# Softmax attentions of a decoder kernel: the last head group's scores go to three pairs of PSUM banks in turn

## The reference, cut to what matters

```python
# L0 xattn: causal self attention (512 keys) + cross attention (1024 keys), heads of 16
y = softmax(mask(q @ k.T) / sqrt(16)) @ v   +   softmax(cq @ ck.T / sqrt(16)) @ cv
x = x + y @ Wp + bp
# L1 xattn: a1 (512 keys, the mask is applied after the softmax), a2 (1024 keys), heads of 32
a = softmax(q @ k.T * 32 ** -0.5);  if causal: a = a * (key > query)
o = a @ v
```

## Time and profile before

| | us |
|---|---|
| median of 3 runs | 3880.21 |
| the runs | 3872.55, 3880.21, 3882.26 |
| the profiled execution: its time | 3883.62 |
| the profiled execution: its span in the trace | 3881.9 |
| mean granted TensorE clock | 0.933 of full speed |
| TensorE / VectorE / ScalarE / GpSimd busy | 3298.2 / 2075.1 / 1646.2 / 918.5 |

### The profile page before, as it was taken

How to read it: one execution, slowest core, us unless ns; L and a number is a source line. 1 busy time by engine, 2 the same in 40 slices (tenths; PEclk the granted TensorE clock), 3 DMA queues, 4 the chain that set the end, 5 groups by cost and what they waited for, 6 DMA issues and landing times. The chain is left out here.

```text
span 3881.9 us, 57542 instructions
## 1 busy us (share of the span) xinstructions
PE 3298.2 (85%) x22048; PEld 1811.7 (47%) x22048; DVE 2075.1 (53%) x4294; ACT 1646.2 (42%) x2481; POOL 918.5 (24%) x966
## 2 busy tenths in 40 slices
PE   6898788898897788898897788999897888985997
PEld 4325445245335545244335535254335635254997
DVE  5665754644656665635656664635656664732111
ACT  3353933343354833333344742433455642431332
POOL 1202912011203712011204622011105622023111
PEclk9999799899998899899998899999998898996999
DMA  4103012111203012011202022011212022025997
GB/s 122 56 15 82 1 47 77 37 33 45 57 13 82 1 47 93 21 38 48 62 18 65 1 47 93 21 39 47 62 44 39 1 47 92 21 88 190 327 329 243
DMA packets 250149, 270.70 MB, mean 70 GB/s; under 512 B 96198, under 2 KB 215988, under 8 KB 247572
## 3 DMA queue, kind: packets, MB, share of 16 engines
q1 hardware_dynamic: 202288, 207.46, 18.2%
q10 hardware_dynamic: 44180, 50.17, 4.1%
q0 software_dynamic: 3408, 9.34, 0.6%
HBM read 199.87 MB, written 67.05 MB: 69 GB/s over the span
## 5 line engine op out<-in xcount | busy, mean ns | idle before, releaser
L881 ACT ACTIVATE prob<-psum 128x1024 f32<-128x1024 f32 x384 | 372.3, 1021 | 514.2 <-PE psum L799 514.2
L1262 ACT ACTIVATE prob<-psum 128x1024 f32<-128x1024 f32 (+3 forms) x384 | 331.2, 914 | 363.4 <-PE psum L1151 363.4
L927 DVE TENSOR_REDUCE scr<-psum 128x1 f32<-128x512 f32 x576 | 369.5, 686 | 201.4 <-PE psum L786 197.4
L1304 DVE TENSOR_REDUCE stats<-psum 128x1 f32<-128x512 f32 (+3 forms) x576 | 332.1, 619 | 139.3 <-PE psum L1139 136.2
L796 PE MATMUL psum<-stack 32*128 32x512 f32 x1536 | 226.6, 660 | 15.2 <-ACT prob L881 10.4
L412 PE MATMUL psum<-ident 128*128 128x128 f32 x1792 | 217.9, 277 | 2.7 <-ACT stack L2229 2.7
L412 PEld LDWEIGHTS psum<-ident 128*128 128x128 f32 x1792 | 210.0, 192 | 15.0 <-issue 7.5
L1139 PE MATMUL psum<-stack 96*128 96x512 bf16 (+3 forms) x576 | 181.3, 363 | 31.5 <-DVE stats L1304 31.2
L829 PE MATMUL psum<-prob,ones_f 128*32 128x512 f32 x1536 | 204.9, 601 | 0.0
L1166 PE MATMUL psum<-prob,vbig 128*32 128x512 f32 (+3 forms) x1536 | 189.4, 566 | 0.0
L1699 POOL TENSOR_TENSOR xo<-xa,rows 128x256 f32<-128x256 f32 x32 | 22.3, 728 | 664.3 <-POOLq L1452 664.3
(11 more groups left out here) (488 smaller groups left out, 6401.5 us busy)
## 6 DMA issues: line engine op xcount, KB each, us to landing
ew<-in_L_ffn_W SPq DMA_DIRECT2D x39, 1024.0 KB
ew<-in_L_ffn_W ACTq DMA_DIRECT2D x39, 1024.0 KB
stack<-q_terms SPq DMA_DIRECT2D x144, 128.0 KB, 2.6
w_mlp<-in_L_xattn_a_li_w SPq DMA_DIRECT2D x16, 1024.0 KB, 6.5
q_terms<-parts SPq DMA_DIRECT2D x96, 128.0 KB, 2.2
stack<-k_terms SPq DMA_DIRECT2D x72, 128.0 KB, 3.0
stack<-k_terms SPq DMA_DIRECT2D x36, 256.0 KB
w_mlp<-a_terms SPq DMA_DIRECT2D x36, 256.0 KB, 4.6
```

The source lines that it names most:

```text
L881: act.activation(prob[:, i % 4, :, :], psum[:, 2 * p:2 * p + 2, :], ACT.Exp, scale=scale).then_inc(exped, 1)
L927: dve.tensor_reduce(found[:, c:c + 1], ring(i), AX.X, ALU.max).then_inc(freed, 1)
L1262: act.activation(prob[:, i % 4, :, q0:T], psum[:, 2 * p:2 * p + 2, q0:T], ACT.Exp, scale=scale).then_inc(exped, 1)
L1304: dve.tensor_reduce(found[:, c:c + 1], ring(i)[:, 0:keys_of(t)], AX.X, ALU.max).then_inc(freed, 1)
```

## The change

In the last head group of all four attentions the scores of step m (counted from the group's first) go by pairs of banks: pair (2m + p) mod 3 for the pair of heads p = 0, 1, where the pairs are banks 0-1, 2-3 and 4-5. A score of this group after its first waits for one exponential of the step before in place of two. Since banks 4 and 5 are taken by that, the products in Bca go to banks 6 and 4 in place of 4 and 5, are ordered by row tile, and are issued at other places: two each at kt = 4, 5 and 6, two before the last gather, two before the last spread, two after it, with two `keep_running` matmuls behind in place of six. They wait for the division of group 2 in place of that of group 1. Cq reads banks 6 and 4, and its transposes use banks 5 and 7.

```diff
+    def score_bank(n, j, kts):
+        m = n - (HG - 1) * kts
+        return j if m < 0 else 2 * ((2 * m + j // 2) % 3) + j % 2
+
+    def exps_before_score(n, kts):
+        return 2 * n if n <= (HG - 1) * kts else 2 * n - 1
...
                     if n:
-                        pe.wait_ge(exped, 2 * n)
+                        pe.wait_ge(exped, exps_before_score(n, kts))
...
-                        last = pe.matmul(psum[:, j, q0:T], KTg[W * j:W * j + W, g, kt * P:(kt + 1) * P],
+                        last = pe.matmul(psum[:, score_bank(n, j, kts), q0:T], KTg[W * j:W * j + W, g, kt * P:(kt + 1) * P],
...
-                    if next_products and g == HG - 1 and 3 <= kt < 7:
-                        pe.wait_ge(divided, HG - 2)
-                        for t, k in next_products[2 * kt - 6:2 * kt - 4]:
+                    if next_products and g == HG - 1 and 4 <= kt < 7:
+                        pe.wait_ge(divided, HG - 1)
+                        for t, k in next_products[2 * kt - 8:2 * kt - 6]:
                             join_attention(pe, t, k)
...
-                if next_products:
-                    pe.wait_ge(divided, HG - 1)
-                for t, k in next_products[8:10]:
+                for t, k in next_products[6:8]:
                     join_attention(pe, t, k)
                 if not next_products:
                     keep_running(pe, 3, 3)
                 gather(HG - 1)
-                for t, k in next_products[10:]:
+                for t, k in next_products[8:10]:
                     join_attention(pe, t, k)
                 if not next_products:
                     keep_running(pe, 2, 3)
                 spread_inverses(pe, HG - 1, inverted, spread_in)
-                keep_running(pe, 6, 3)
+                for t, k in next_products[10:]:
+                    join_attention(pe, t, k)
+                keep_running(pe, 2 if next_products else 6, 3)
...
-                        act.activation(prob[:, i % 4, :, q0:T], psum[:, 2 * p:2 * p + 2, q0:T], ACT.Exp,
+                        b0 = score_bank(n, 2 * p, kts)
+                        act.activation(prob[:, i % 4, :, q0:T], psum[:, b0:b0 + 2, q0:T], ACT.Exp,
...
-        return pe.matmul(psum[:, 4 + t // 2, t % 2 * C:(t % 2 + 1) * C], yT[:, k, t * P:(t + 1) * P], wBp[:, k, :],
+        return pe.matmul(psum[:, (6, 4)[t // 2], t % 2 * C:(t % 2 + 1) * C], yT[:, k, t * P:(t + 1) * P], wBp[:, k, :],
...
-                   next_products=[(t, k) for k in range(HG - 1) for t in range(QT)], beside=add_bias)
+                   next_products=[(t, k) for t in range(QT) for k in range(HG - 1)], beside=add_bias)
...
-        return psum[:, 4 + h, :].rearrange("p (t n) -> p t n", t=2)
+        return psum[:, (6, 4)[h], :].rearrange("p (t n) -> p t n", t=2)
...
-                turn(h, 6 + h).then_inc(turned, 1)
+                turn(h, 5 + 2 * h).then_inc(turned, 1)
```

More of the change, by code:

```diff
@@ L795, in score @@
                     for j in range(J):
-                        pe.matmul(psum[:, j, :], KTg[W * j:W * j + W, g, kt * P:(kt + 1) * P], QTg[W * j:W * j + W, g, :],
+                        pe.matmul(psum[:, score_bank(n, j, kts), :], KTg[W * j:W * j + W, g, kt * P:(kt + 1) * P], QTg[W * j:W * j + W, g, :],
                                   start=True, stop=False)
                     for j in range(J):
-                        last = pe.matmul(psum[:, j, :], ones_b[W * j:W * j + W, :], low[W * j:W * j + W, g % 2, :],
+                        last = pe.matmul(psum[:, score_bank(n, j, kts), :], ones_b[W * j:W * j + W, :], low[W * j:W * j + W, g % 2, :],
                                          start=False, stop=True)
@@ L880, in _ @@
                             act.wait_ge(weighed, n - 1)
-                        act.activation(prob[:, i % 4, :, :], psum[:, 2 * p:2 * p + 2, :], ACT.Exp, scale=scale).then_inc(exped, 1)
+                        b0 = score_bank(n, 2 * p, kts)
+                        act.activation(prob[:, i % 4, :, :], psum[:, b0:b0 + 2, :], ACT.Exp, scale=scale).then_inc(exped, 1)
                     if kt == order[0] and g:
@@ L2219, in _ @@
                 pe.wait_ge(normed, 2 * QT - 2 + 2 * h)
-                turn(h, 6 + h).then_inc(x_turned, 1)
+                turn(h, 5 + 2 * h).then_inc(x_turned, 1)
             e.keep_running(pe, 6, 0)
@@ L2233, in _ @@
                 act.wait_ge(turned, h + 1)
-                act.copy(xT[:, :, h * N:(h + 1) * N], psum[:, 6 + h, :].rearrange("p (k n) -> p k n", k=KT)).then_inc(xT_in, 1)
+                act.copy(xT[:, :, h * N:(h + 1) * N], psum[:, 5 + 2 * h, :].rearrange("p (k n) -> p k n", k=KT)).then_inc(xT_in, 1)
             for h in range(2):
                 act.wait_ge(x_turned, h + 1)
-                act.copy(xT[:, :, h * N:(h + 1) * N], psum[:, 6 + h, :].rearrange("p (k n) -> p k n", k=KT))
+                act.copy(xT[:, :, h * N:(h + 1) * N], psum[:, 5 + 2 * h, :].rearrange("p (k n) -> p k n", k=KT))
         @block.gpsimd
```

## The result

The changed kernel took 3852.11 us (median of 5 runs, 3840.52 to 3860.08) against 3882.26 us before (median of 5). The ratio is 0.9926 with a 95% interval of 0.9905 to 0.9947: faster by 30 us. The profiled execution is the slowest of the five: 3860.08 us, its span 3858.2, beside 3881.9 before. Later runs of the same kernel gave 3840.83 and 3841.71 us (ratios 0.9891 and 0.9901), so the first measurement stands at the upper end of what this kernel takes.

A forecast was written before the change was run, and what follows sets the result against it. In the last head groups, ScalarE waits for scores held behind both exponentials, with TensorE's own work a second limit. 7.19 us a sequence, 28.8 in all, 31.2 with the clock: 3880.2 - 31.2 = 3849 us, range 3838 to 3866.

The forecast's parts named there:

- The count of idle time ahead of the scores: Last groups: each step gains TensorE's idle time ahead of the scores; e2 1.75, e1 1.45, Ba 1.07, Bca 2.92 us.
- a forecast of 74 us: All 20 last-group steps of a sequence give the full 0.92 us: 73.6 us in all, 3807 us; chance 0.02.
- Bca, 2.92: Bca's last group, 7 steps: three gain 0.92 us, two gain 0.08, two with products nothing; 2.92 us a sequence.
- weigh to scores: Bca's last group: TensorE's distance from weigh to scores, taken as 1.07 us by its duration.
- The mask: Ba and e1 last groups: weigh waits for the mask, about 0.1 us in e1, until about 141.5 in Ba.
- The products' new wait: Bca: the wait for group 2's division has cover, over some 2.7 us after the spread's start, behind three sets of 1.07.
- their new places: Bca: two new products behind the spread, 1.06 us, run beside the last division; counted at nothing, at most 4 us in all.
- Rival 1: Scores come early everywhere because TensorE has more slack than the rows show: 73.6 us gained, 3807 us; chance 0.02.
- Rival 3: In 80 last-group steps overlapped scores and exponentials slow each other; at 0.89 us a step 3922 us, slower; chance 0.04.
- Rival 4: The gain is absorbed behind the stages, or the wait was not the last one: 3880 us; chance 0.05.
- Rival 2: The clock falls more often, each of the 16 last groups catching a low stretch: 21.4 us lost, 3873 us; chance 0.07.
- the clock: Last groups of Ba and Bca: low-clock stretches worth 4.8 us; half of that, 2.4 us, counted as gained.

The follow-up runs named there:

- `products_only`: Changed kernel with its new products and Cq's banks, but scores in banks 0 to 3 waiting for both exponentials as before: 3883.08 us, ratio 0.9999.
- `two_later`: Changed kernel with the two products of kt = 4 moved behind the last spread, no identity matmuls there: 3843.38 us, 0.9909 of before.
- `four_later`: Changed kernel with the products of kt = 4 and 5 moved behind the last spread, no identity matmuls there: 3838.76 us, 0.9896 of before.
- `banks_only`: Changed kernel, three pairs of banks kept, but last-group scores wait for both exponentials as before: 3880.51 us, 1.0002 of before.

## Why the prediction was right

3849 us was forecast, within 3838 to 3866, and 3852.11 measured, 30.2 us less than before for 31.2.

- **The count of idle time ahead of the scores.** It held in each stage, to 0.03 us a sequence in Ba, e1 and e2. That the full 0.92 of an exponential is given only where TensorE has nothing else to do was the point on which a forecast of 74 us and one of 29 part.
- **Bca, 2.92 for 3.08.** The term mis-sized is weigh to scores: 1.07 was read off the modelled duration, and the start-to-start distance is 1.00 (297.01 to 298.01), so steps with products take 3.12 and not 3.20, and the one with the gather 3.05 and not 3.12; only the one with the spread, 3.15, is longer than forecast. For e2 the distance had been taken from starts, and there it fits.
- **The mask.** In Ba TensorE idles 0.51 us for it ahead of `weigh`, and 1.04 were gained for 1.07; in e1 the step that waits is 3.30, for 3.39 before and 3.27 by the working.
- **The products' new wait and their new places** cost nothing that shows in `products_only`. The expectation of `two_later` put the cover at about 1.5 us, which is too short: in `four_later` the six products take 2.75 us and 0.70 of it shows, so some 2.05 are covered, 0.4 of it behind the end of the division.
- **Rival 1**, the scores early everywhere, is excluded by the 3.14 in e2. **Rival 3**, that scores and exponentials slow each other, by the 1.21 us from scores to exponential with and without overlap, and by exponentials of e1 and e2 that are nowhere longer than 1032 ns in the first profile and 1036 in any other. **Rival 4**, that the gain is absorbed behind the stages, is excluded for e1 and Bca: from e1's last exponential to e2's first it takes 85.7 us in the mean with both versions, and from Bca's last to the next stage's first sum 9.9. Behind Ba and e2 the shortest stretches are alike in both versions (35.9 and 115.4 us), but behind Ba the mean is longer by 0.7 us a sequence, so there the rival is right in part.
- **Rival 2 and the clock.** The size, 2.4 us, came out near the sum by chance, and the account behind it was incomplete. The stretches in the last groups went altogether, 4.7 us of them and not half, so the fear that bank cycling makes the clock swing was unfounded here. What stood low before the change stood where TensorE idled up to 1.7 us ahead of the scores, 16 of 48 last groups of Ba and Bca. The Trainium skill (TensorE: Matmul & The Clock Gate, "A second HAM failure mode: psum-queue depth-cycling") expects swings where TensorE cycles through banks with short idle times; the trace does not agree, the granted clock is 1.00 in the last groups of all 32 sequences of Ba and Bca profiled with the change. The prediction's argument against this rival, that the granted clock is full where TensorE is nearly always busy, does not hold everywhere: 0.57 over 31.92 us with TensorE busy 28.78 of them. And I looked for the clock only where the change is. It acted elsewhere, in both directions: 18.9 us lost at the start of Bca in the profiled execution, 7.5 us gained in the mean at the start of e2, 2.7 lost behind Ba.

The mean of the three measurements of the changed kernel is some 36 us below before. The terms are 29.1 for the steps, 3.0 for the mean of the low-clock stretches of the last groups (8.25 - 7.81 and 23.61 - 23.31 a sequence, four times) and 7.5 for e2's start, less 2.7 behind Ba, less 3.0 behind the last e2 (453.7 us to the end in the mean with the old `narrow_heads`, 456.6 with the new one), and less up to 3 for the stretches at Bca's start if these are more frequent at all: 31 to 34. What is left open, 2 to 5 us, is no more than the medians of one kernel differ by. The profiles say the same: the mean span of the three of the changed kernel is 33 us below that of `before`, `banks_only` and `products_only`; the last groups make up 33 of it, and what the clock gives and takes elsewhere cancels. Only the 29.1 us are shown by experiments to be the change's; that the forecast of the total came within 1 us is partly luck. Why one measurement gave 3852 and two gave 3841 stays open; the clock goes with it, 0.932 in the mean of the five runs above 3850 us, 0.938 in that of the ten others.

## What to carry to other kernels

When a buffer is turned round faster, the gain of a step is the idle time of the producer ahead of it and not the length of what is overlapped; read it from the distance of starts, in each stage by itself, since the modelled end of a matmul hides a few hundredths. Work that is moved out of a full queue is free only as long as something else ends later; here about 0.4 us of that cover lay behind the last division, in the handover to the next stage. When parts of a change measured alone don't add up to the whole, compare stretches in which nothing was changed: here the granted clock at the start of two stages moved the time by 18.9 us in one execution and by 7.5 us in the mean, beside 29.1 us from the change.

## What was not expected of the hardware

- TensorE stayed at 1.2 GHz for 27.3 us on end within a stretch of 31.92 us of which it was busy 28.78, in work that runs at the full clock in the other sequences.
- With e1 and e2 ending 1.4 and 1.7 us earlier, the unchanged start of e2 spends less time at the lower clock: in sequence 0 it was 10.5 us before and 1.1 after, for 113.57 and 109.98 us of the same instructions. That the earlier ends are the cause is not shown.
- Scores written into four banks by four row tiles while exponentials are read from others slowed neither: 1.21 us from scores to exponential with and without the overlap, and exponentials of 1016 to 1032 ns for 1015 to 1032.
